# Contraction over pairs of time steps, and a scan's carry added by TensorE

## The chip, the cores and the metric

The kernel runs on one NeuronCore of a Trainium2 chip. The metric is the device time of one execution in microseconds (us). A core has five engines that run at the same time and wait for each other through semaphores: TensorE (PE, matmuls, with its weight loads shown as PEld), VectorE (DVE), ScalarE (ACT), GpSimd (POOL) and SyncE (SP), which here issues all DMAs. SBUF is the memory on the core with 128 partitions; PSUM is where PE writes, in 8 banks of 512 float32 per partition; PE adds there. GpSimd and DMA do not reach PSUM.

## The reference

Two layers with residuals over x of 4 x 1024 x 256 float32. The first is a selective scan:

```python
x = x + selective(layernorm(x))
# in selective, for batch b, channel d (256), state n (32), time t (1024):
dA    = exp(delta_t[:, :, None] * A[None])
dBu   = (delta_t * u_t)[:, :, None] * B_t[:, None, :]
h     = dA * h + dBu
y_t   = einsum('bdn,bn->bd', h, C_t)
...
y     = ys + u * D_param
```

delta, B and C come from projections of the normalised x. The second layer (`x + ffn(layernorm(x))`) has a two-tap convolution with SiLU, projections to queries, keys, values and gates, a routed attention whose length axis is the batch of four, a normalisation and an output projection.

## The kernel before

It has three stages. The first (P, to about 222 us) makes delta, delta times u, B and C, splits float32 numbers into bfloat16 terms and stores them in DRAM, with `base` = x + u D. The second (M, to about 850 us) is the scan. The third (F) is the second layer, over 8 tiles of 128 time steps.

In stage M the 128 partitions hold batch x state (4 x 32). Time goes in 32 chunks of 32 (`TC`); a chunk has two halves (`s`) of 16 time steps (`TS`), and a half has four groups `g` of 64 channels. One of these groups is called a step here: 8 a chunk, 256 in all, G being the step's number. Each step does this:

- PE, L1313: 8 bfloat16 matmuls write dBu for 64 channels x 16 time steps into one of two pairs of PSUM banks. They wait for the scan two steps back (L1308), which read that pair. `b_ready` counts them.
- PE, L1269 (`decay_args`): 8 bfloat16 matmuls write delta A for the next chunk. ACT takes the exponential (L1406) into `decay`.
- PE, L1282 (`contract`): y = C h for a half already scanned. The state is laid out channel by channel with the 16 time steps of a half adjacent, so that one time step of all 256 channels is a row of elements 16 apart. Each matmul takes one time step `t`: its stationary operand is 32 columns of `c_sta` (C of that time step, in 4 of the 32 columns, the rest zero), its output one of four 32-row blocks of PSUM, block `j` = t mod 4. Four of them run per step, side by side in the array. The columns of `c_sta` are placed so that row 4 q + b of block j gets time step 4 q + j of batch b; 8 rounds q accumulate over a chunk.
- POOL, L1163: `carry` = first decay of the step times the last state of the same channels in the half before. It waits for the scan four steps back. Then L1166 sets that first decay to 0, since one scan instruction runs over all 64 channels in a row.
- DVE, L1582: adds `carry` to the first time step of each channel in PSUM, and waits for itself. Then L1585: the scan over 64 x 16 elements.

Once a chunk POOL fills `c_sta` (L1140), ACT copies y from PSUM to `y_rows` (L1434), and SP stores it (`store_y`, L1032) with four DMAs, one for each block, as rows of 256 channels into `y_d`, which is laid out as batch, time, channel. SP also loads the inputs of the chunk after next (`load_md`, `load_mu`).

In stage F SP loads a tile of y and a tile of `base` with one DMA each (`f_load`, L295). POOL adds them (L368, `x1`), and later does gates (L380) and sums (L389) in the same queue. `phase_f_sync` gives the order on SP: the load of tile lt + 4, then the wait for tile lt's result and its store, then the load of tile lt + 5. The order within every engine is that of the code; nothing reorders it.

## Time and profile before

| | |
|---|---|
| device time, 3 runs | 1081.23, 1082.9, 1084.27 us (median 1082.9) |
| profiled execution, its own time | 1081.63 us |
| span of the profile | 1079.9 us |
| PE, DVE busy in the span | 85%, 81% |
| ACT, POOL busy in the span | 42%, 36% |
| mean granted clock of PE | 0.899 of full |

The span runs from the first to the last instruction of one profiled execution. A float32 matmul appears as two records (two passes), a bfloat16 one as one. In a view in order of time a row stands for several instructions of one line: its start, the time from the first start to the last end, and their count. Ends of matmuls overlap the next one, so the distance between two starts tells how long PE was taken. A granted clock of 1.00 is 2.4 GHz, 0.50 is 1.2 GHz.

### The profile page before, as it was taken

The page shows a single profiled execution, that of the slowest core. Times are in us where ns is not written, and L with a number is a line of the kernel's source. Part 1 is how long each engine was busy: PE and PEld are TensorE (multiplying, and loading weights), DVE is VectorE, ACT ScalarE, POOL GpSimd, SP SyncE. Part 2 cuts the span into 40 slices and gives each one's busy share as a digit, 9 for nine tenths or more (in the row PEclk, how much of TensorE's full clock was granted, in tenths as well). Part 3 has the DMA queues.
Part 4 walks back from the last instruction along what each step waited for, and adds up shares of the span by engine and source line. Part 5 has one row for each costly group of instructions (what it writes and reads, how often), then busy time and mean ns, then how long its engine had stood idle before and what let it go on. Part 6 is the DMA issues. An engine that isn't in the chain of part 4 may idle for free.

```text
span 1079.9 us, 22889 instructions
## 1 busy us (share of the span) xinstructions
PE 919.4 (85%) x7472; PEld 591.4 (55%) x7472; DVE 873.3 (81%) x1116; ACT 458.6 (42%) x807; POOL 384.4 (36%) x698
## 2 busy tenths in 40 slices
PE   5655462469999999999999999999999699777996
PEld 3433241346666666666666666666665377556774
DVE  6844575079999999999999999999999758455773
ACT  3444644424444444444444444444443244222531
POOL 6434643123333333333333333333335442333232
PEclk9655665579999999999999999999999999888997
DMA  9399998771121121111111211112114210111001
GB/s 327 59 152 175 209 130 138 125 125 59 53 63 53 52 65 53 60 58 51 63 54 50 65 53 60 56 53 63 53 51 143 70 58 1 59 59 59 21 20 59
DMA packets 206074, 85.76 MB, mean 79 GB/s; under 512 B 139221, under 2 KB 196053, under 8 KB 205269
## 3 DMA queue, kind: packets, MB, share of 16 engines
q1 hardware_dynamic: 206036, 85.30, 33.8%
q8 instruction: 19, 0.31, 0.1%
q14 instruction: 19, 0.15, 0.0%
HBM read 45.85 MB, written 39.42 MB: 79 GB/s over the span
## 4 chain that ended last, share of the span: by engine, by line
PE 63%; SPq 15%; issue 8%; DVE 7%; POOL 4%; ACT 2%; DMA 1%; ACTq 0%; POOLq 0%; DVEq 0%
PE psum L1282 23%; PE psum L1313 21%; PE psum L1269 10%; SPq L957 6%; SPq L1010 5%; PE psum L442 5%; DVE arena L1585 3%; POOL arena L389 2%; SPq L974 1%; PE psum L514 1%; SPq L951 1%; POOL arena L380 1%; PE psum L510 1%; POOL arena L368 1%; DMA delta_terms<-arena 0%
## 5 line engine op out<-in xcount | busy, mean ns | idle before, releaser
L1585 DVE TENSOR_TENSOR_SCAN arena<-arena,psum 128x1024 f32<-128x1024 f32 x256 | 585.4, 2287 | 8.8
L1406 ACT ACTIVATE arena<-psum 128x512 f32<-128x512 f32 x512 | 281.5, 604 | 349.6 <-PE psum L1269 308.0
L1313 PEld LDWEIGHTS psum<-du_mov,b_sta 96*128 96x128 bf16 x2048 | 200.3, 130 | 239.0 <-issue 214.1
L1313 PE MATMUL psum<-du_mov,b_sta 96*128 96x128 bf16 x2048 | 271.8, 313 | 20.2 <-DVE arena L1585 20.1
L1282 PE MATMUL psum<-arena,c_sta 128*32 128x256 f32 x2048 | 280.7, 629 | 2.3 <-DVE arena L1585 2.1
L1163 POOL TENSOR_TENSOR carry<-arena 128x64 f32<-128x64 f32 x252 | 119.0, 472 | 393.3 <-DVE arena L1585 384.6
L1269 PE MATMUL psum<-delta_mov,a_sta 96*128 96x128 bf16 x2048 | 171.7, 228 | 10.6 <-DMA delta_mov<-delta_terms 7.7
L1269 PEld LDWEIGHTS psum<-delta_mov,a_sta 96*128 96x128 bf16 x2048 | 151.9, 110 | 13.8 <-issue 8.1
L442 PE MATMUL psum<-delta_mov,arena 128*128 128x256 f32 (+6 forms) x544 | 119.9, 381 | 7.2 <-ACT arena L567 7.2
L442 PEld LDWEIGHTS psum<-delta_mov,arena 128*128 128x128 f32 x544 | 93.6, 205 | 28.4 <-ACT arena L567 8.2
L1582 DVE TENSOR_TENSOR psum<-psum,carry 128x64 f32<-128x64 f32 x256 | 55.1, 215 | 38.2 <-DMA delta_terms<-arena 38.2
L1166 POOL TENSOR_TENSOR arena<-zeros 128x64 f32<-128x64 f32 x256 | 78.1, 305 | 20.1
L1225 PE MATMUL psum<-arena 128*64 128x512 f32 x32 | 29.1, 1067 | 49.9 <-ACT arena L1354 49.9
L1282 PEld LDWEIGHTS psum<-arena,c_sta 128*32 128x32 f32 x2048 | 40.8, 108 | 31.5 <-issue 3.1
L811 DVE TENSOR_TENSOR arena<-arena 128x1024 f32<-128x1024 f32 x8 | 20.9, 2611 | 39.3 <-POOL arena L380 39.3
L1119 POOL TENSOR_TENSOR arena<-c_sta,arena 128x1024 f32<-128x1024 f32 x8 | 18.5, 2308 | 66.3 <-ACT arena L1393 66.3
L368 POOL TENSOR_TENSOR arena<-du_mov 128x1024 f32<-128x1024 f32 x8 | 18.8, 2356 | 64.5 <-DMA du_mov<-base 64.5
L1463 DVE BATCH_NORM_STATS2 arena<-arena 128x6 f32<-128x256 f32 x32 | 11.2, 410 | 37.6 <-DMA arena<-in_L_attn_x 37.6
L691 DVE TENSOR_TENSOR arena<-arena,psum 128x512 f32<-128x512 f32 (+3 forms) x32 | 14.5, 483 | 32.1 <-ACT delta_mov L583 19.1
L1225 PEld LDWEIGHTS psum<-arena 128*64 128x64 f32 x32 | 5.9, 213 | 62.7 <-ACT arena L1354 52.7
L389 POOL TENSOR_TENSOR arena<-arena 128x768 f32<-128x768 f32 (+2 forms) x24 | 36.0, 1500 | 8.9 <-DVE arena L745 6.6
L602 ACT ACTIVATE arena<-arena 128x1024 f32<-128x1024 f32 x8 | 8.5, 1057 | 63.9 <-POOL arena L389 63.9
(142 smaller groups left out, 777.1 us busy)
## 6 DMA issues: line engine op xcount, KB each, us to landing
du_terms<-arena SPq DMA_DIRECT2D x48, 256.0 KB, 3.9
du_mov<-du_terms SPq DMA_DIRECT2D x128, 96.0 KB
b_terms<-delta_mov SPq DMA_DIRECT2D x6, 1024.0 KB, 10.5
delta_terms<-arena SPq DMA_DIRECT2D x48, 128.0 KB, 5.2
delta_mov<-delta_terms SPq DMA_DIRECT2D x128, 48.0 KB
b_sta<-b_terms SPq DMA_DIRECT2D x64, 96.0 KB
arena<-in_L_attn_x SPq DMA_DIRECT2D x8, 512.0 KB, 5.6
base<-arena SPq DMA_DIRECT2D x8, 512.0 KB, 4.6
```

The source lines that it names most:

```text
L389: pool.tensor_tensor(o[:, 0:n], o[:, 0:n], arena[:, AV_TMP[m]:AV_TMP[m] + n], ALU.add)\
L442: mm = nc.tensor.matmul(psum[:, at:at + n], xc, w_all[:, h * WCOLS + col:h * WCOLS + col + n], start=(h == 0), stop=(h == 1))
L957: sp_.dma_start(dram(scratch_d, s * per_term + offset, *dims_), part(which)).then_inc(count, 16)
L1010: sp_.dma_start(dram(delta_terms_d, s * (B * L * D) + lt * (B * P * D) + h * (P * TC), (TC, P), (TC * D, B * P // TC), (1, TC)), dp_view(k ...
L1163: ins = pool.tensor_tensor(carry[:, g, :], seg[:, :, 0], before[:, :, TS - 1], ALU.mult)
L1166: pool.tensor_tensor(seg[:, :, 0], zeros[:, :], zeros[:, :], ALU.add)\
L1269: mm = nc.tensor.matmul(psum[:, (4 + u % 2) * BANK + i * P:(4 + u % 2) * BANK + (i + 1) * P], a_sta[0:ROWS, dg * P:(dg + 1) * P], sub(delt ...
L1282: mm = nc.tensor.matmul(psum[32 * j:32 * j + 32, (6 + k) * BANK:(6 + k) * BANK + D], c_sta[k][:, t * 32:(t + 1) * 32], sub(arena, 0, P, (2 ...
L1313: mm = nc.tensor.matmul(sub(psum, 0, P, o, (4, 4), (TS, GD // 2)), b_sta[k][0:ROWS, (s * 4 + tg) * P:(s * 4 + tg + 1) * P], sub(du_mov[k], ...
L1406: nc.scalar.activation(sub(arena, 0, P, k * CHUNK_ELEMS + u * 16 * TS, (TS, 16), (D * TS, SUBS), (1, TS)), sub(psum, 0, P, (4 + u % 2) * B ...
L1582: nc.vector.tensor_tensor(firsts, firsts, carry[:, g, :], ALU.add)\
L1585: nc.vector.tensor_tensor_scan(state[s][:, seg], decay[k][:, (s * D + g * GD) * TS:(s * D + (g + 1) * GD) * TS], psum[:, 2 * (step % 2) * ...
```

## The change

Three things are changed.

1. `contract` takes two adjacent time steps in one matmul (`TP` = 2): 512 columns, two adjacent elements out of every 16, with one stationary operand of 32 columns. Output block j of PSUM now holds two times 256 columns. A half has 2 rounds of 4 matmuls, where it had 4; they are placed in steps g = 1 and g = 3. A chunk has 4 rounds p. The matmul of round p and block j takes time steps 8 p + 2 j + u, u = 0 and 1. Its stationary operand holds C of both, in columns 8 p + 4 u + b for batch b, the rest zero; its output has two groups of 256 columns, one for each of the two states. So row 8 p + 4 u + b of block j holds y of its time step in column group u; what the other group holds there is not used. POOL fills `c_sta` with two operations (L1148 of the changed kernel), one for each u, with half the elements each.
2. y is copied whole (512 columns) and stored with one DMA a chunk, 128 rows of 2 KB, unused parts included. `f_load` picks the used parts with eight DMAs, each to 16 partitions 8 apart, and one for `base` (`YLOADS` = 9).
3. The carry is added by PE: after the 8 matmuls of L1313 (whose loops change places, halves outside) it waits for `carry_ready` and adds `carry` by two float32 matmuls with the identity as stationary operand, 32 columns each, in PSUM. DVE's addition and the semaphore `carried` go.

```diff
+TP = 2
+SETS = TS // (4 * TP)
+YROW = TP * D
+YLOADS = 4 * TP + 1
-        y_d = scratch("y", [B, L, D], F32)
+        y_d = scratch("y", [4, CHUNKS * 32, TP, D], F32)
-        y_rows = [sb(f"y_rows{k}", [P, D]) for k in range(2)]
+        y_rows = [sb(f"y_rows{k}", [P, 2 * D]) for k in range(2)]
...
         def f_load(eng, lt, k):
-            for tile, source in ((fraw[k], y_d), (fbase[k], base_d)):
-                eng.dma_start(tile.rearrange("p (b d) -> p b d", b=B),
-                              dram(source, lt * (P * D), (D, P), (L * D, B), (1, D))).then_inc(f_loaded[k], 16)
+            for j in range(4):
+                for u in range(TP):
+                    eng.dma_start(sub(fraw[k], TP * j + u, 16, 0, (D, B), (1, D), pstep=4 * TP),
+                                  dram(y_d, (j * CHUNKS * 32 + lt * P + u * B) * YROW + u * D,
+                                       (TP * B * YROW, 16), (YROW, B), (1, D))).then_inc(f_loaded[k], 16)
+            eng.dma_start(fbase[k].rearrange("p (b d) -> p b d", b=B),
+                          dram(base_d, lt * (P * D), (D, P), (L * D, B), (1, D))).then_inc(f_loaded[k], 16)
...
             def store_y(c, k):
-                for j in range(4):
-                    sp_.dma_start(dram(y_d, c * (TC * D) + j * D, (4 * D, TC // 4), (L * D, B), (1, D)),
-                                  y_rows[k][32 * j:32 * j + 32, :]).then_inc(y_stored[k], 16)
+                sp_.dma_start(dram(y_d, c * (32 * YROW), (CHUNKS * 32 * YROW, 4), (YROW, 32), (1, YROW)),
+                              y_rows[k][:, :]).then_inc(y_stored[k], 16)
...
-                    pool.tensor_tensor(
-                        sub(c_sta[k], 0, P, 0, (4 * 32 + 4, TC // 4), (32, 4), (1, B)),
+                    for u in range(TP):
+                        pool.tensor_tensor(
+                            sub(c_sta[k], 0, P, u * B, (4 * 32 + TP * B, 4), (32, 4), (1, B)),
...
                             if not early:
+                                pool.wait_ge(S["b_ready"], G - 3)
                                 pool.wait_ge(S["scan_done"], G - 3)
-                                pool.wait_ge(S["carried"], G - 3)
...
-            def contract(c, k, s, quads):
-                for qq in quads:
+            def contract(k, s, sets):
+                for r in sets:
                     for j in range(4):
+                        pi = SETS * s + r
                         mm = nc.tensor.matmul(
-                            psum[32 * j:32 * j + 32, (6 + k) * BANK:(6 + k) * BANK + D],
-                            c_sta[k][:, t * 32:(t + 1) * 32],
-                            sub(arena, 0, P, (2 * CHUNK_ELEMS + s * D * TS) + 4 * qq + j, (TS, D)),
+                            psum[32 * j:32 * j + 32, (6 + k) * BANK:(6 + k) * BANK + TP * D],
+                            c_sta[k][:, (pi * 4 + j) * 32:(pi * 4 + j + 1) * 32],
+                            sub(arena, 0, P, (2 * CHUNK_ELEMS + s * D * TS) + TP * (4 * r + j), (TS, D), (1, TP)),
...
-                            for tg in range(TS // 4):
-                                for half in range(2):
+                            for half in range(2):
+                                for tg in (1, 2, 3, 0):
...
+                            pe.wait_ge(S["carry_ready"], G + 1)
+                            for half in range(2):
+                                mm = nc.tensor.matmul(
+                                    sub(psum, 0, P, (pair_bank + half) * BANK, (TS, GD // 2)), ident[:, :],
+                                    carry[:, g, half * (GD // 2):(half + 1) * (GD // 2)],
+                                    start=False, stop=True, skip_group_check=True)
                             mm.then_inc(S["b_ready"], 1)
...
-                                if g == 0:
-                                    pe.wait_ge(S["scan_done"], G)
+                                if g == 1:
+                                    pe.wait_ge(S["scan_done"], G - 1)
...
-                                mm = contract(pc, pk, ps, [g])
+                                if g % 2 == 1:
+                                    mm = contract(pk, ps, [g // 2])
...
-                            firsts = sub(psum, 0, P, 2 * (step % 2) * BANK, (TS, GD))
-                            nc.vector.tensor_tensor(firsts, firsts, carry[:, g, :], ALU.add)\
-                                .then_inc(S["carried"], 1)
-                            dve.wait_ge(S["carried"], G + 1)
```

On PE, two steps of a chunk's inner loop, before (L1313 the inputs, L1269 the arguments, L1282 the contraction; REGISTER_ALU rows compute what a wait compares):

```order
L1313 MATMUL psum<-du_mov,b_sta 128x4x32 x8
L1266 REGISTER_ALU
L1269 MATMUL psum<-delta_mov,a_sta 128x128 x4
L1266 REGISTER_ALU
L1269 MATMUL psum<-delta_mov,a_sta 128x128 x4
L1282 MATMUL psum<-arena,c_sta 32x256 x4
L1308 REGISTER_ALU
L1313 MATMUL psum<-du_mov,b_sta 128x4x32 x8
L1266 REGISTER_ALU
L1269 MATMUL psum<-delta_mov,a_sta 128x128 x4
```

And in the changed kernel, where these are L1320, L1277 and L1289, and L1327 are the identity matmuls on `carry`:

```order
L1320 MATMUL psum<-du_mov,b_sta 128x4x32 x8
L1325 REGISTER_ALU
L1327 MATMUL psum<-carry,ident 128x32 x2
L1274 REGISTER_ALU
L1277 MATMUL psum<-delta_mov,a_sta 128x128 x4
L1274 REGISTER_ALU
L1277 MATMUL psum<-delta_mov,a_sta 128x128 x4
L1289 MATMUL psum<-arena,c_sta 32x512 x4
L1320 MATMUL psum<-du_mov,b_sta 128x4x32 x8
L1325 REGISTER_ALU
L1327 MATMUL psum<-carry,ident 128x32 x2
```

The contraction stands in every second step with twice the columns, and two identity matmuls stand behind the inputs in every step.

On SP, the end of stage M and the beginning of stage F, before (L1032 stores y, L295 loads y and base):

```order
L1032 DMA y<-y_rows 8x4x256 x4
L295 DMA du_mov<-y 128x4x256
L295 DMA du_mov<-base 128x4x256
L295 DMA du_mov<-y 128x4x256
L295 DMA du_mov<-base 128x4x256
L1032 DMA y<-y_rows 8x4x256 x8
```

And in the changed kernel (L1039 the store, L300 and L303 the loads):

```order
L1039 DMA y<-y_rows 4x32x512
L300 DMA du_mov<-y 16x4x256 x8
L303 DMA du_mov<-base 128x4x256
L300 DMA du_mov<-y 16x4x256 x8
L303 DMA du_mov<-base 128x4x256
L1039 DMA y<-y_rows 4x32x512 x2
```

A store has one DMA where it had four, a tile's load nine where it had two.

## Rows read from the trace of the kernel before

**Rows 1.** The page's first part: busy time, share of the span, instructions of each engine.

```profile
PE 919.4 (85%) x7472; PEld 591.4 (55%) x7472; DVE 873.3 (81%) x1116; ACT 458.6 (42%) x807; POOL 384.4 (36%) x698
```

**Rows 2.** Stages: us, then busy time (instructions) by engine, granted clock, DMA share, GB/s.

```profile
222.30:262.00 39.70, 37.19 (x341) 24.95 (x344) 39.11 (x34) 16.16 (x31) 12.69 (x33) 0.89 0.31 94
262.00:830.00 568.00, 568.00 (x5558) 342.46 (x5551) 560.03 (x463) 262.22 (x493) 191.57 (x529) 1.00 0.18 58
830.00:850.40 20.40, 17.48 (x137) 8.27 (x135) 20.12 (x18) 1.15 (x3) 15.45 (x28) 1.00 0.31 103
```

**Rows 3.** Lines, 300 to 800 us: form, count, busy us, mean ns, idle before.

```profile
L1585 DVE TENSOR_TENSOR_SCAN arena<-arena,psum 128x1024 f32<-128x1024 f32 x205 | 468.8, 2287 | 7.1
...
L1282 PE MATMUL psum<-arena,c_sta 128*32 128x256 f32 x1632 | 224.1, 629 | 0.0
...
L1269 PE MATMUL psum<-delta_mov,a_sta 96*128 96x128 bf16 x1632 | 132.9, 224 | 0.0
```

**Rows 4.** Order of time, 502 to 505 us: start, us, what, count, idle before.

```profile
502.03 0.43 POOL L1163 TENSOR_TENSOR carry<-arena 128x64 f32<-128x64 f32 x1 [1.63 <-DVE arena L1585]
...
502.11 2.29 DVE L1585 TENSOR_TENSOR_SCAN arena<-arena,psum 128x1024 f32<-128x1024 f32 x1
502.11 1.08 PE L1282 MATMUL psum<-arena,c_sta 128*32 128x256 f32 x8
...
503.13 1.05 PE L1313 MATMUL psum<-du_mov,b_sta 96*128 96x128 bf16 x8
...
503.97 0.65 PE L1269 MATMUL psum<-delta_mov,a_sta 96*128 96x128 bf16 x8
504.31 0.21 DVE L1582 TENSOR_TENSOR psum<-psum,carry 128x64 f32<-128x64 f32 x1
...
504.55 1.12 PE L1282 MATMUL psum<-arena,c_sta 128*32 128x256 f32 x8
504.56 2.29 DVE L1585 TENSOR_TENSOR_SCAN arena<-arena,psum 128x1024 f32<-128x1024 f32 x1
```

**Rows 5.** Other float32 matmuls on PE in order of time, then the clock there.

```profile
66.05 3.67 PE L1225 MATMUL psum<-arena 128*64 128x512 f32 x4 [7.64 <-ACT arena L1354]
69.65 1.10 PE L1234 MATMUL psum<-arena 128*32 128x128 f32 x16
70.69 1.97 PE L1240 MATMUL psum<-arena 128*128 128x32 f32 x16
...
945.38 1.88 PE L510 MATMUL psum<-arena,ident 128*128 128x512 f32 x4
947.10 3.62 PE L514 MATMUL psum<-delta_mov,arena 128*128 128x256 f32 x16
...
69.60:70.60 1.00, 1.00 (x17) 0.65 (x16) 0.00 (x0) 0.58 (x1) 0.00 (x0) 0.50 0.98 320
70.68:72.70 2.02, 1.98 (x20) 1.86 (x16) 0.93 (x3) 0.00 (x0) 0.00 (x0) 1.00 1.14 164
```

**Rows 6.** PE in order of time, two groups of the first steps.

```profile
226.28 1.14 PE L1269 MATMUL psum<-delta_mov,a_sta 96*128 96x128 bf16 x8
227.22 1.91 PE L1313 MATMUL psum<-du_mov,b_sta 96*128 96x128 bf16 x8
```

**Rows 7.** PE in order of time, the contraction behind the last scan.

```profile
850.43 3.90 PE L1282 MATMUL psum<-arena,c_sta 128*32 128x256 f32 x32 [0.41 <-DVE arena L1585]
```

**Rows 8.** A load of the last stage; then SP's issues, ns min/median/max.

```profile
952.27 0.51 SPq L295 DMA_DIRECT2D du_mov<-y  x1
...
958.69 2.34 POOL L368 TENSOR_TENSOR arena<-du_mov 128x1024 f32<-128x1024 f32 x1 [18.97 <-DMA du_mov<-base]
...
L295 SPq DMA_DIRECT2D du_mov<-y x8: 367/474/507, 828.1 to 982.5; - x8
...
DMA to landing us min/median/max: 3.5/5.8/7.3
...
L1032 SPq DMA_DIRECT2D y<-y_rows x128: 656/677/790, 253.1 to 856.9; - x128
```

More of the change, by code:

```diff
@@ L122, in bank @@
             return psum[:, i * BANK:(i + n) * BANK]
[L125 removed]
+        names = """own_made b_filled a_sta_zeroed c_sta_zeroed wv_sum wv_mean
             wv_centred weights_loaded ident_zeroed ident_ready zeros_ready wT_psum wT_ready a_exp a_neg a_hi
@@ L277, in m_done @@
             for k in range(2):
-                eng.wait_ge(y_stored[k], 16 * 4 * (CHUNKS // 2))
+                eng.wait_ge(y_stored[k], 16 * (CHUNKS // 2))
         def dims(t, off, *d):
@@ L364, in x1 @@
             def x1(lt):
-                pool.wait_ge(f_loaded[lt % 2], 32 * (lt // 2 + 1))
+                pool.wait_ge(f_loaded[lt % 2], 16 * YLOADS * (lt // 2 + 1))
                 if lt >= FY:
@@ L1139, in m_pair @@
                         pool.wait_ge(S["contract_done"], 2 * c - 2)
-                    pool.tensor_tensor(
-                        sub(c_sta[k], 0, P, 0, (4 * 32 + 4, TC // 4), (32, 4), (1, B)),
-                        c_all[:, bass.ds(c * TC, TC)].rearrange("p (q j) -> p q j", j=4)
-                        .unsqueeze(3).to_broadcast([P, TC // 4, 4, B]),
-                        sub(own_batch, 0, P, 0, (0, TC // 4), (0, 4), (1, B)), ALU.mult)\
-                        .then_inc(S["cpad_ready"], 1)
+                    for u in range(TP):
+                        pool.tensor_tensor(
+                            sub(c_sta[k], 0, P, u * B, (4 * 32 + TP * B, 4), (32, 4), (1, B)),
+                            c_all[:, bass.ds(c * TC, TC)].rearrange("p (q j u) -> p q j u", j=4, u=TP)[:, :, :, u]
+                            .unsqueeze(3).to_broadcast([P, 4, 4, B]),
+                            sub(own_batch, 0, P, 0, (0, 4), (0, 4), (1, B)), ALU.mult)\
+                            .then_inc(S["cpad_ready"], 1)
                     for s in range(SUBS):
@@ L1274, in decay_args @@
                 return mm
-            def contract(c, k, s, quads):
-                for qq in quads:
+            def contract(k, s, sets):
+                for r in sets:
                     for j in range(4):
-                        t = s * TS + 4 * qq + j
-                        q = t // 4
+                        pi = SETS * s + r
                         mm = nc.tensor.matmul(
-                            psum[32 * j:32 * j + 32, (6 + k) * BANK:(6 + k) * BANK + D],
-                            c_sta[k][:, t * 32:(t + 1) * 32],
-                            sub(arena, 0, P, (2 * CHUNK_ELEMS + s * D * TS) + 4 * qq + j, (TS, D)),
-                            start=(q == 0), stop=(q == TC // 4 - 1), skip_group_check=True)
+                            psum[32 * j:32 * j + 32, (6 + k) * BANK:(6 + k) * BANK + TP * D],
+                            c_sta[k][:, (pi * 4 + j) * 32:(pi * 4 + j + 1) * 32],
+                            sub(arena, 0, P, (2 * CHUNK_ELEMS + s * D * TS) + TP * (4 * r + j), (TS, D), (1, TP)),
+                            start=(pi == 0), stop=(pi == SETS * SUBS - 1), skip_group_check=True)
                 return mm
@@ L1337, in _ @@
             pe.wait_ge(S["scan_done"], CHUNKS * STEPS)
-            contract(CHUNKS - 1, 1, 1, range(4)).then_inc(S["contract_done"], 1)
+            contract(1, 1, range(SETS)).then_inc(S["contract_done"], 1)
             phase_f_pe(pe)
@@ L1409, in exps, with y_copy @@
                     .then_inc(S["exp_done"], 1)
+            def y_copy(k):
+                nc.scalar.copy(y_rows[k].rearrange("p (u d) -> p u d", u=TP),
+                               sub(psum, 0, P, (6 + k) * BANK, (1, TP), (TP, D))).then_inc(S["y_evac"], 1)
             for u in range(UNITS):
@@ L1432, in m_pair @@
                             if not (isinstance(n, int) and n <= 0):
-                                act.wait_ge(y_stored[1 - k], 64 * n)
-                            nc.scalar.copy(y_rows[1 - k][:, :],
-                                           bank(7 - k)[:, 0:D])\
-                                .then_inc(S["y_evac"], 1)
+                                act.wait_ge(y_stored[1 - k], 16 * n)
+                            y_copy(1 - k)
             m_pair(0, True, False)
@@ L1445, in _ @@
             act.wait_ge(S["contract_done"], 2 * CHUNKS)
-            act.wait_ge(y_stored[1], 64 * (CHUNKS // 2 - 1))
-            nc.scalar.copy(y_rows[1][:, :], bank(7)[:, 0:D]).then_inc(S["y_evac"], 1)
+            act.wait_ge(y_stored[1], 16 * (CHUNKS // 2 - 1))
+            y_copy(1)
             phase_f_act(act)
```

5 lines of the change are left out of this document (2 added, 3 removed).

## The prediction, made before the changed kernel was run

> **What bounds the kernel now.** I read the page's first part, then the stages, the costliest lines, and the order of time inside one step. The page gives PE 85% and DVE 81% of a 1079.9 us span [rows 1]. The stages show where: from 262 to 830 us PE is busy 568.00 of 568 and DVE 560.03, at the full clock (2.4 GHz), while ACT and POOL are under half and DMA takes 0.18 [rows 2]. So this is a loop with two nearly full engines, and 85% against 81% does not say which of them sets the pace. The lines from 300 to 800 us hold 204 steps, 2.451 us each (500/204), each with one scan of 2287 ns [rows 3].
>
> Inside a step [rows 4]: scan starts 502.11, next L1582 starts 504.31, next scan 504.56. A scan therefore holds DVE for 2.20 us, and the addition with its wait for itself costs 0.25. DVE shows no idle time. PE starts the contraction at 502.11, the state inputs (L1313) at 503.13, the exponents' arguments (L1269) at 503.97 and the next contraction at 504.55: 1.02, 0.84 and 0.58, no gap between them. Over many steps the contraction averages 2.451 − 0.84 − 0.58 = 1.03. Both engines sum to 2.45: taking work from DVE alone would gain nothing, PE's new sum decides. ACT is under half full; POOL computes a carry right after a scan (502.03), for a scan four steps later.
>
> **DVE.** 256 additions leave. DVE's floor becomes 2.20 a step.
>
> **PE, what goes.** Half a chunk (four steps) had four groups of four contractions over 256 columns, each a matmul in two passes; now two groups over 512, in every second step. What a 512-column pass takes is the disputed number. In one group (32 matmul records, four groups, eight passes in 3.90 us) a 256-column pass takes (3.90 − 0.63)/7 = 0.47 [rows 7, 3]; in the loop, from the x8 row, (1.08 − 0.63) = 0.45 [rows 4]. Other float32 matmuls at full clock: L514, 256 adjacent columns, 3.62/16 = 0.23, a little less without the last record's overhang; L510, 512 columns, (947.10 − 945.38)/4 = 0.43 [rows 5]. The contraction's columns thus cost double. It differs in two ways: four 32-column tiles run side by side, and it picks one element out of every 16 (64 bytes). The tiles are not the cause as far as a row shows: L1234 runs four tiles of 128 adjacent columns in (70.69 − 69.65)/4 = 0.26, and L1225 at the same half clock (granted 0.50) needs (69.65 − 66.05)/4 = 0.90 for 512 columns in one stream, 0.23 for 128 [rows 5]. So the stride is what is left. The change reads two adjacent elements per 64 bytes. No row shows that form: a 512-column pass lies between 0.43 (adjacent) and 0.90 (as now). I take 0.43 plus the 0.03 that a pass carries now (0.46), because the doubling looks like one extra access time per separate piece, and there are half as many pieces. A group then costs what it costs today, 1.03, and there are half as many. At the upper end it costs 1.03 + 2 × 0.43 = 1.89.
> The Trainium skill, "SBUF — State Buffer", section "Door 1: The DMA port swizzle", says that SBUF lines are 16 bytes long and that at least two accesses to a line are needed for full bandwidth. By that rule one element per 64 bytes is slow and two adjacent ones are at full speed (a group of 1.03); without it, nothing but my reading of the stride supports the halving (1.89 remains possible). Its penalty for single elements agrees with 0.45 against 0.23.
>
> **PE, what comes.** Two identity matmuls of 32 columns per step, two passes each, so four weight loads of 128 × 128 float32. L1240 has this very form at the full clock: 16 records in 1.97, the last about 0.28 long, so 1.69/15 = 0.113 [rows 5]. Four are 0.45. I take 0.43, since the last of the L1313 matmuls already holds PE for 0.11 while the first identity is loaded. Bounds: 0.11, if loads were hidden and only the columns counted (4 × 32 columns at 0.23/256); 0.86, if each pass took what a 256-column one takes. The writes go to PSUM 64 bytes apart, as those of L1313, which cost 0.84/8 = 0.11 per 128 against 0.06 for L1269; for 32 columns that stays below the load. The order of L1313 (halves outside) moves nothing: the same eight loads and writes; between 0 and a doubled 0.11 each I take 0. The new wait, for the carry, sits ahead of the identity matmuls, and behind it are the arguments and the contraction, for which ACT and DVE wait. POOL has the carry ready about 0.5 after the scan four steps back, and the inputs wait for a scan two steps back, so it costs nothing. In the last chunk POOL also turns keys between carries, which eats into a lead of two steps but not all of it; a loss there would be a step or so, and I take 0.
>
> **The step.** Arguments before a contraction cost 0.58; without one behind them 8 × 0.061 = 0.49 (0.65 less the last record's 0.22 [rows 3, 4], over 7). Two steps: 0.84 + 0.43 + 0.49 + 0.84 + 0.43 + 0.58 + 1.03 = 4.64, so 2.32 per step against DVE's 2.20. PE is then the bound. The contraction in one lump does not stall it: the input for a step may start when the scan two back is over. Count from the start of an even step's input: its scan starts at 0.84 + 0.43 + 0.28 = 1.55, the odd one's 2.20 later at 3.75, so the odd scan before that started at −0.89 and ended at 1.40, and PE comes to the odd input only at 1.76. All 256 steps but the first four and the last eight run in this form: 244 × (2.451 − 2.323) = −31.2.
>
> **The ends.** (1) The first four steps run at half clock: an input group takes about 1.6 and arguments 227.22 − 226.28 = 0.94 [rows 6]; with about 0.5 more PE is behind DVE, +0.4. (2) The last seven intervals have no arguments, PE needs 2.32 less about 0.5 and DVE sets them: 7 × 0.25 = −1.7. (3) The last contraction, on the chain, took 3.90 for four groups [rows 7]; two remain, −1.9, and its copy to `y_rows` is twice as wide, +0.2. (4) In the last stage SP loads y and base for tile lt + 4 only behind the output of tile lt. POOL sits idle for 18.97 us until base lands, and the gates and sums behind it go through POOL [rows 8]; tiles 5, 6 and 7 all wait like this, so three loads are on the path. From y's issue to x1 is 6.4 (952.27 to 958.69). Now there are eight y issues ahead of base's. One issue lies between 0.37 and 0.68 in the rows [rows 8]; I take 0.45 and 0.04 between, so base starts 3.9 after instead of 0.55. It no longer shares the engines with a whole y: a load alone landed in as little as 3.5 [rows 8], so 3.9 + 3.6 = 7.5 and a loss of 1.1, at worst (0.68 each) 2.9, at best 0. With what the issue of base itself may add I take 1.5, three times, and 0.5 for tile 2: +5.0. SP's y stores fall from four to one a chunk; it was not the bound. ACT's wider copy (0.2 more) and POOL's second c_sta operation fit in their idle time.
>
> Sum: 1081.6 (the profiled execution, 1.7 over its span, 1.3 under the median of 1082.9, inside their range) − 31.2 + 0.4 − 1.7 − 1.7 + 5.0 = 1052.4, say **1052**.
>
> **Rivals.** *Pairs read no faster.* A group costs 1.89 and two steps 5.50, 2.75 each: 244 × 0.30 = +73; the last intervals −1.2, the tail +0.1, first steps and loads as above: **1159**, slower. For it: every strided read of state here has the same stride, so nothing separates piece from element. Against: adjacent columns run at twice the rate. It decides from a group of 1.27 (passes of 0.58), where the whole comes out even. *Identity matmuls dearer*, 0.86 instead of 0.43: 2.75 per step, about **1157**; half of that is 1105. For it: float32 weights between bfloat16 ones occur nowhere in the loop. Against: L1240 is the same form. *They are hidden*: with 0.19 or less a step PE sums under 2.20 and DVE sets it: −61, **1023**. For it: L1313 is slow for another reason than weights, so loads might slip beneath. Against: L1240 shows loads as the rate at 32 columns.
>
> **Numbers.** Forecast 62% (its own range 1035 to 1073, from 0.36 to 0.52 for the identity passes), hidden 13%, pairs no faster 14%, dearer identities 11%. The range 1018 to 1095 holds the forecast, the hidden case and the mild part of dearer identities; pairs without gain are left out. About 3 us either way, 0.3%, cannot be told from no change here. Faster: 62 + 12; same: 4, from the mild dear case; slower: 22.
>
> **What would show it.** After the change: steps of 4.6 in pairs; 512-column passes of 0.46 (right) or 0.9 (wrong); the input start to the arguments start 1.27 instead of 0.84; DVE idle about 0.1 a step waiting for PE, where before it had none; DVE without idle time means the hidden case. In the last stage POOL's waits for base grow by 1 to 2 us each. A granted clock below full in the loop would make the prediction wrong, as would PE waiting on POOL's carry.

## The result, and the profile after

| | before | after |
|---|---|---|
| device time, median (lowest to highest) | 1083.59 us (1081.23 to 1086.44), 4 runs | 1052.51 us (1050.63 to 1056.41), 4 runs |
| ratio of after to before, 95% interval | | 0.9717 [0.9678, 0.9756] |
| the profiled execution | 1081.63 us, span 1079.9 | 1050.63 us, span 1048.9 |

Executions over 1.5% above the fastest of the same kernel are left out of the ratios, here and in the experiments. 31.0 us left the profiled execution. The page's first part for the kernel after, with each engine's busy time and its share of the span (before: [rows 1]):

```profile
PE 883.2 (84%) x7472; PEld 672.1 (64%) x7472; DVE 824.1 (79%) x860; ACT 462.5 (44%) x807; POOL 379.6 (36%) x730
```

PE lost 36 us of work and DVE 49, and both shares look as before; where the time went is to be read from the stages. Loop and first steps of the kernel after; the columns are those of [rows 2] (duration, busy time of PE, PEld, DVE, ACT and POOL, granted clock, DMA share, GB/s):

```profile
222.30:262.00 39.70, 38.82 (x338) 31.90 (x338) 34.04 (x16) 15.68 (x29) 12.15 (x34) 0.80 0.28 84
262.00:800.00 538.00, 537.21 (x5632) 415.64 (x5632) 525.33 (x237) 266.49 (x494) 195.73 (x576) 1.00 0.24 71
```

In the loop PE is full, as before, and DVE now has 12.7 us of idle time in 538. PE is the bound. The costliest lines from 300 to 780 us (before: [rows 3]), with count, busy time, mean ns of one, idle time ahead and who ended it:

```profile
L1597 DVE TENSOR_TENSOR_SCAN arena<-arena,psum 128x1024 f32<-128x1024 f32 x211 | 470.4, 2273 | 11.5 <-PE psum L1327 5.9
...
L1289 PE MATMUL psum<-arena,c_sta 128*32 128x512 f32 x840 | 121.0, 640 | 0.0
L1327 PE MATMUL psum<-carry,ident 128*128 128x32 f32 x844 | 120.7, 266 | 0.0
```

The scan is what it was. The identity matmuls have as much busy time as the whole contraction, which has 105 groups of 8 passes. Two steps in order of time (before: [rows 4]):

```profile
500.13 6.73 DVE L1597 TENSOR_TENSOR_SCAN arena<-arena,psum 128x1024 f32<-128x1024 f32 x3 [0.23 <-PE psum L1327]
...
500.21 1.04 PE L1320 MATMUL psum<-du_mov,b_sta 96*128 96x128 bf16 x8
...
501.05 0.57 PE L1327 MATMUL psum<-carry,ident 128*128 128x32 f32 x4
...
501.45 0.61 PE L1277 MATMUL psum<-delta_mov,a_sta 96*128 96x128 bf16 x8
...
502.00 1.12 PE L1289 MATMUL psum<-arena,c_sta 128*32 128x512 f32 x8
...
503.05 1.05 PE L1320 MATMUL psum<-du_mov,b_sta 96*128 96x128 bf16 x8
...
503.89 0.57 PE L1327 MATMUL psum<-carry,ident 128*128 128x32 f32 x4
...
504.30 0.61 PE L1277 MATMUL psum<-delta_mov,a_sta 96*128 96x128 bf16 x8
...
504.75 0.71 PE L1320 MATMUL psum<-du_mov,b_sta 96*128 96x128 bf16 x5
```

From start to start on PE: inputs 0.84, identities 0.40, arguments 0.55, contraction 1.05 over 512 columns, then inputs 0.84, identities 0.41 and arguments 0.45. DVE runs three scans without a gap and waited 0.23 for the identity matmuls ahead of them. Over many steps a group takes 1.055 or 1.116, 1.085 in the mean, and two steps are 4.57.

Marked by the starts of the scans, the profiled executions differ as follows. An interval is the time from one scan's start to the next one's; the forecast of a row is the prediction's terms laid on the same marks (0.128 gained in each of 244 intervals, 8 of them in the second row and 8 in the fourth).

| | before | after | difference | forecast |
|---|---|---|---|---|
| to the first scan | 222.34 | 220.84 | −1.5 | 0 |
| first 12 intervals | 29.44 | 32.58 | +3.1 | −0.6 |
| next 228 intervals | 2.454 each | 2.283 each | −39.0 | −29.2 |
| last 15 intervals | 36.75 | 33.54 | −3.2 | −2.7 |
| last scan to the end | 231.83 | 241.35 | +9.5 | +3.3 |
| sum | | | −31.0 | −29.2 |

The first row lies ahead of the loop that the change touches; over all the profiles here it varies from 217.8 to 225.0 with no order by kernel, so it is the spread of single executions. Of the others the loop gave 10 us more than forecast, and the two ends took 10 back.

**First steps.** In the kernel after, in order of time:

```profile
226.41 1.92 PE L1320 MATMUL psum<-du_mov,b_sta 96*128 96x128 bf16 x8
...
228.04 0.98 PE L1327 MATMUL psum<-carry,ident 128*128 128x32 f32 x4
...
228.83 1.04 PE L1277 MATMUL psum<-delta_mov,a_sta 96*128 96x128 bf16 x8
...
229.66 1.92 PE L1320 MATMUL psum<-du_mov,b_sta 96*128 96x128 bf16 x8
...
235.63 2.29 DVE L1597 TENSOR_TENSOR_SCAN arena<-arena,psum 128x1024 f32<-128x1024 f32 x1 [0.94 <-PE psum L1327]
...
236.31 1.94 PE L1289 MATMUL psum<-arena,c_sta 128*32 128x512 f32 x8
```

And the clock there (columns as above):

```profile
230.00:236.00 6.00, 6.00 (x39) 6.00 (x38) 4.07 (x3) 1.66 (x5) 1.96 (x6) 0.50 0.17 53
236.00:238.00 2.00, 2.00 (x12) 0.31 (x10) 1.92 (x1) 1.07 (x2) 0.00 (x0) 0.50 0.00 0
238.00:262.00 24.00, 24.00 (x254) 18.77 (x250) 21.89 (x10) 11.34 (x21) 7.99 (x22) 0.99 0.22 65
```

A step takes 3.25 (226.41 to 229.66): 1.63 for the inputs, 0.79 for the identities, 0.83 for the arguments, with no gap on PE, and the scan waits 0.94 for it. The granted clock is 0.50 (1.2 GHz) until 238 us, although PE is busy without a break from 223.2 on. In the kernel before PE was busy from 224.7 on, with no gap over 0.15, and the clock rose at 231.1 (0.74 in the mean of 230 to 232).

**Last stage.** SP and POOL after the output of tile 1, in order of time (before: [rows 8]):

```profile
913.98 0.38 SPq L318 DMA_DIRECT2D out<-arena  x1
914.41 5.33 SPq L300 DMA_DIRECT2D du_mov<-y  x8
...
919.78 0.59 SPq L303 DMA_DIRECT2D du_mov<-base  x1
924.14 2.34 POOL L376 TENSOR_TENSOR arena<-du_mov 128x1024 f32<-128x1024 f32 x1 [22.30 <-DMA du_mov<-base]
```

From the store of a tile to the `x1` that waits for the load behind it (the load of tile 5 stands behind the store of tile 0, and so on) are 10.9, 10.2 and 10.0 us for tiles 5, 6 and 7, and were 8.3, 6.8 and 7.0.

### The profile page after: what moved, and what is told of

It reads as the page before. It is cut to its first block, busy times and chain, and to the rows that moved or that the text cites. A ratio compares the mean times of both kernels' runs of the same rounds, so it can differ in the third digit from the quotient of the medians.

```text
span 1048.9 us, 22555 instructions
## 1 busy us (share of the span) xinstructions
PE 883.2 (84%) x7472; PEld 672.1 (64%) x7472; DVE 824.1 (79%) x860; ACT 462.5 (44%) x807; POOL 379.6 (36%) x730
## 4 chain that ended last, share of the span: by engine, by line
PE 65%; SPq 15%; issue 9%; DVE 4%; POOL 4%; ACT 2%; DMA 1%; ACTq 0%; POOLq 0%; DVEq 0%
PE psum L1320 22%; PE psum L1289 13%; PE psum L1277 11%; PE psum L1327 9%; SPq L965 6%; PE psum L450 6%; SPq L1018 5%; POOL arena L397 2%; DVE arena L1597 2%; SPq L982 1%; PE psum L522 1%; SPq L959 1%; PE psum L518 1%; POOL arena L388 1%; POOL arena L376 1%
## 5 line engine op out<-in xcount | busy, mean ns | idle before, releaser
L1597 DVE TENSOR_TENSOR_SCAN arena<-arena,psum 128x1024 f32<-128x1024 f32 x256 | 570.6, 2273 | 58.0 <-DMA delta_terms<-arena 39.6
L1420 ACT ACTIVATE arena<-psum 128x512 f32<-128x512 f32 x512 | 278.1, 595 | 308.3 <-PE psum L1277 304.5
L1320 PEld LDWEIGHTS psum<-du_mov,b_sta 96*128 96x128 bf16 x2048 | 206.2, 131 | 136.1 <-DVE arena L1597 133.2
L1320 PE MATMUL psum<-du_mov,b_sta 96*128 96x128 bf16 x2048 | 272.1, 314 | 19.0 <-DVE arena L1597 19.0
L1171 POOL TENSOR_TENSOR carry<-arena 128x64 f32<-128x64 f32 x252 | 110.8, 440 | 361.5 <-DVE arena L1597 270.8
L1277 PE MATMUL psum<-delta_mov,a_sta 96*128 96x128 bf16 x2048 | 163.2, 224 | 12.5 <-DMA delta_mov<-delta_terms 9.7
L1277 PEld LDWEIGHTS psum<-delta_mov,a_sta 96*128 96x128 bf16 x2048 | 143.9, 110 | 15.7 <-issue 10.0
L1327 PE MATMUL psum<-carry,ident 128*128 128x32 f32 x1024 | 148.8, 269 | 0.0
L1327 PEld LDWEIGHTS psum<-carry,ident 128*128 128x128 f32 x1024 | 148.1, 206 | 0.0
L1289 PE MATMUL psum<-arena,c_sta 128*32 128x512 f32 x1024 | 148.0, 643 | 0.0
L450 PE MATMUL psum<-delta_mov,arena 128*128 128x256 f32 (+6 forms) x544 | 119.7, 380 | 7.1 <-ACT arena L575 7.1
L450 PEld LDWEIGHTS psum<-delta_mov,arena 128*128 128x128 f32 x544 | 93.6, 205 | 28.9 <-issue 8.9
L376 POOL TENSOR_TENSOR arena<-du_mov 128x1024 f32<-128x1024 f32 x8 | 18.8, 2351 | 74.9 <-DMA du_mov<-base 74.8
L511 PE MATMUL psum<-ident,arena 128*128 128x128 f32 x64 | 11.9, 349 | 34.5 <-DVE arena L819 33.2
```

The source lines that it names most:

```text
L450: mm = nc.tensor.matmul(psum[:, at:at + n], xc, w_all[:, h * WCOLS + col:h * WCOLS + col + n], start=(h == 0), stop=(h == 1))
L1171: ins = pool.tensor_tensor(carry[:, g, :], seg[:, :, 0], before[:, :, TS - 1], ALU.mult)
L1277: mm = nc.tensor.matmul(psum[:, (4 + u % 2) * BANK + i * P:(4 + u % 2) * BANK + (i + 1) * P], a_sta[0:ROWS, dg * P:(dg + 1) * P], sub(delt ...
L1289: mm = nc.tensor.matmul(psum[32 * j:32 * j + 32, (6 + k) * BANK:(6 + k) * BANK + TP * D], c_sta[k][:, (pi * 4 + j) * 32:(pi * 4 + j + 1) * ...
L1320: mm = nc.tensor.matmul(sub(psum, 0, P, o, (4, 4), (TS, GD // 2)), b_sta[k][0:ROWS, (s * 4 + tg) * P:(s * 4 + tg + 1) * P], sub(du_mov[k], ...
L1327: mm = nc.tensor.matmul(sub(psum, 0, P, (pair_bank + half) * BANK, (TS, GD // 2)), ident[:, :], carry[:, g, half * (GD // 2):(half + 1) * ...
```

## Experiments

Each line number in an edit is that of the kernel after or before that it starts from; a run with one time is a single execution, and the kernel before took 1084.8 us in a single execution beside the first four.

**1. What makes the contraction cheap: adjacent elements, one 16-byte piece, or neither?** `arena` holds 4 bytes an element, so the two elements of a pair lie in one aligned 16-byte piece. Three kernels change only which two elements a matmul reads, so their y is not the reference's. In e3_across_line blocks 2 and 3 read the same elements, and both rounds of a half read the same.

```diff
-  sub(arena, ..., TP * (4 * r + j), (TS, D), (1, TP)),
+  sub(arena, ..., 4 * r + j, (TS, D), (8, TP)),              # e1_apart: 32 bytes apart
+  sub(arena, ..., 4 * j + r, (TS, D), (2, TP)),              # e2_same_line: 8 apart, one piece
+  sub(arena, ..., 4 * min(j, 2) + 3, (TS, D), (1, TP)),      # e3_across_line: adjacent, two pieces
```

> The changed kernel, but the two time steps of a contraction lie 8 elements (32 bytes) apart instead of side by side; 512 columns as before. y comes from other time steps than it should. Theory A (a column costs double when it stands alone in its 16 bytes): a 512-column pass takes 0.9 us instead of the 0.46 of the changed kernel, a group 1.9 to 2.0, two steps 4.57 + 0.86 = 5.43, and the time rises by 122 x 0.86 = 105 us to about 1157 us. Theory B (the old contraction was slow because of its many small groups and tiles side by side, not because of its stride): the pass stays at 0.46 and the time at 1052 us.

> The changed kernel, but the two time steps of a contraction are elements 0 and 2, or 1 and 3, of an aligned group of four (same 16 bytes, not adjacent). y comes from other time steps than it should. Theory A (16 bytes count): as fast as adjacent ones, a pass 0.46 us, the time 1052 us. Theory C (adjacency counts, a separate piece costs double): a pass 0.9 us, the time about 1157 us.

> The changed kernel, but the two time steps of a contraction are adjacent elements on either side of a 16-byte border (3 and 4, 7 and 8, 11 and 12). y comes from other time steps than it should. Theory A (16 bytes count): a pass 0.9 us, the time about 1157 us. Theory C (adjacency counts): a pass 0.46 us, the time 1052 us.

Measured: 1159.48, 1041.24 and 1157.92 us. The contraction and the group behind it on PE, e1_apart first:

```profile
499.84 2.02 PE L1289 MATMUL psum<-arena,c_sta 128*32 128x512 f32 x8
501.79 1.05 PE L1320 MATMUL psum<-du_mov,b_sta 96*128 96x128 bf16 x8
```

Then e2_same_line:

```profile
502.84 1.07 PE L1289 MATMUL psum<-arena,c_sta 128*32 128x512 f32 x8
503.84 1.05 PE L1320 MATMUL psum<-du_mov,b_sta 96*128 96x128 bf16 x8
```

And e3_across_line:

```profile
501.37 2.04 PE L1289 MATMUL psum<-arena,c_sta 128*32 128x512 f32 x8
503.34 1.05 PE L1320 MATMUL psum<-du_mov,b_sta 96*128 96x128 bf16 x8
```

A group takes 1.95, 1.00 and 1.97; from the start of its first matmul record to that of its fifth, which is one pass, are 0.906, 0.457 and 0.867. Adjacency doesn't matter: two elements with a gap between them are fast in one 16-byte piece, and two neighbours across its border are as slow as two that lie apart. So the halving came from the piece, and the first rival ("pairs read no faster") describes just what these two slow kernels do: they sit at its 1159. The rule of the Trainium skill, "SBUF — State Buffer", section "Door 1: The DMA port swizzle", that lines are 16 bytes and want two accesses each, is borne out here for TensorE's moving operand (0.457 against 0.906 and 0.867).

e2_same_line was also 11 us faster than the kernel after. Its pass is a constant 0.457, while that of the kernel after is 0.459 in one group and 0.510 in the next. The difference between the two: in the kernel after, the matmuls of blocks 0 and 1, and those of blocks 2 and 3, read two halves of the same 16 bytes from two tiles of the array, with starts 0.007 apart; in e2_same_line each tile has pieces of its own. Experiment 7 uses that. In the two slow kernels tiles share pieces too; no run here separates that from their pairs being split, but in the kernel after sharing by two tiles costs at most 0.05 a pass, against the 0.41 to 0.45 in question.

**2. What the carry costs on PE, and where DVE's floor is.** The identity matmuls and their wait are left out, and with them the carry from half to half.

```diff
-  pe.wait_ge(S["carry_ready"], G + 1)
-  for half in range(2):
-      mm = nc.tensor.matmul(sub(psum, ...), ident[:, :], carry[:, g, ...], ...)
```

> The changed kernel without the two identity matmuls and their wait: the carry is left out of the scan. PE then needs (4.57 - 2 x 0.41)/2 = 1.88 us a step. Theory A (PE's sum sets the changed kernel's pace of 2.283): DVE takes over at 2.20, the loop gains 244 x 0.08 = 20 us and the slow first steps 3 us more, about 1030 us, with no DVE idle time in the loop. Rival (DVE or POOL already sets the pace): no change, 1050 us.

Measured: 1021.48 us, 2.178 a step, below both the 2.20 and the 1030 us that were expected. DVE and PE in order of time:

```profile
498.44 8.79 DVE L1591 TENSOR_TENSOR_SCAN arena<-arena,psum 128x1024 f32<-128x1024 f32 x4
...
502.94 1.05 PE L1320 MATMUL psum<-du_mov,b_sta 96*128 96x128 bf16 x8 [0.44 <-DVE arena L1591]
```

Now DVE runs without a gap and PE waits for it. This is the forecast's "hidden" case, made real: 1023 was its time. The first 12 intervals take 26.53 instead of 32.58, 6.0 less, of which the loop's gain (12 × 0.105) explains 1.3; the other 4.8 are what the identities cost there, with their own time at the half clock and with a half clock that lasts longer (see the end of the section on the prediction).

**3. Each half of the change alone.** e5_pairs_only is the kernel after with the carry added by DVE as before. e6_carry_only is the kernel before with the carry on PE. The semaphore that POOL's carry waits for changes with them.

```diff
 # e5_pairs_only, from the kernel after
-  (the wait for carry_ready and the two identity matmuls)
+  nc.vector.tensor_tensor(firsts, firsts, carry[:, g, :], ALU.add).then_inc(S["carried"], 1)
+  dve.wait_ge(S["carried"], G + 1)
 # e6_carry_only, from the kernel before: the same lines the other way round
```

> The contraction in pairs and y stored whole, but the carry added by DVE as before. Theory A (before, both engines were full; PE relieved alone gains nothing): DVE stays at 2.20 + 0.24 a step, so 2.44 to 2.45, the last contraction saves 2 us and the y loads of the last stage cost 9: 1083.6 + 5 = 1088 us, 0.4% slower than before. Rival (before, PE set the pace and DVE's additions were slowed by it): the step falls to 2.3 or less and the time to 1055 us.

> The kernel before, with the carry added by PE and the contraction in single time steps, y stored as before. Theory A: PE needs 0.83 + 0.41 + 0.54 + 1.05 = 2.83 us a step, 244 x 0.38 = +93 us and some 4 us in the first steps: about 1178 us. Rival (DVE set the pace before, PE had room that its records hide): not over 1100 us.

Measured: 1087.67 us (1082.68 to 1090.21, 10 runs), ratio 1.0023 [1.0004, 1.0042], for the pairs; 1176.85, ratio 1.0845 [1.0817, 1.0873], for the carry. In e5_pairs_only:

```profile
500.38 0.21 DVE L1592 TENSOR_TENSOR psum<-psum,carry 128x64 f32<-128x64 f32 x1
500.52 1.05 PE L1320 MATMUL psum<-du_mov,b_sta 96*128 96x128 bf16 x8 [0.76 <-DVE arena L1595]
500.62 2.29 DVE L1595 TENSOR_TENSOR_SCAN arena<-arena,psum 128x1024 f32<-128x1024 f32 x1
```

And in e6_carry_only, where L1320 are the identity matmuls:

```profile
501.19 2.29 DVE L1587 TENSOR_TENSOR_SCAN arena<-arena,psum 128x1024 f32<-128x1024 f32 x1 [0.43 <-PE psum L1320]
501.46 1.12 PE L1282 MATMUL psum<-arena,c_sta 128*32 128x256 f32 x8
```

With the pairs alone PE idles (0.76 before the inputs) behind a DVE that still needs 2.45 a step, and the slower last stage (240.97 from the last scan to the end, against 231.83) is what is left. With the carry alone DVE idles behind a PE that needs 2.84. PE's relief is worth nothing without DVE's, and DVE's, bought with work on PE, costs 8% without PE's: the gain is a property of both together. That is what [rows 2] said with two full engines.

**4. The last stage.** e7_one_y_load fetches y with one DMA, as before, of rows that are not the tile's y; everything else is the kernel after.

```diff
-  for j in range(4):
-      for u in range(TP):
-          eng.dma_start(sub(fraw[k], TP * j + u, 16, ...), dram(y_d, ...))
+  eng.dma_start(fraw[k].rearrange("p (b d) -> p b d", b=B), dram(y_d, lt * (P * D), (D, P), ...))
```

> The changed kernel, but in the last stage a tile of y is loaded by one DMA of the same bytes with base's pattern, so it holds the wrong rows. Theory A (the eight small loads cost the three waits of POOL 3 us each): 9 to 10 us less, about 1043 us. Rival (the last stage is longer for another reason, such as the lower clock of its first transposes): 1052 us.

Measured: 1044.52 us, ratio 0.9641 [0.9602, 0.968]. From the last scan to the end it takes 231.99, against 241.35 after and 231.83 before. SP and POOL after the output of tile 1:

```profile
911.54 0.38 SPq L315 DMA_DIRECT2D out<-arena  x1
...
912.51 1.05 SPq L300 DMA_DIRECT2D du_mov<-base  x1
918.34 2.35 POOL L373 TENSOR_TENSOR arena<-du_mov 128x1024 f32<-128x1024 f32 x1 [19.09 <-DMA du_mov<-base]
```

6.8 from the store to `x1`, where it was 10.2. So the eight loads are the whole loss of the last stage, 9.4 us, and the shorter last contraction gave nothing that can be seen there: the result of tile 0 is stored 72.2 us after the start of the last scan in the kernel before (920.31) and after (879.77) alike.

**5. The wait for the load itself.** Both kernels issue the load of tile lt + 5 only behind the output of tile lt. Here every load from tile 4 on is issued two tiles earlier, so those of tiles 4, 5 and 6 stand ahead of the first output.

```diff
   load(3)
+  load(4)
+  load(5)
   for lt in range(LT):
-      if lt + 4 < LT: load(lt + 4)
+      if lt + 6 < LT: load(lt + 6)
```

> The kernel before, with SP issuing the loads of tiles 5, 6 and 7 of the last stage two tiles earlier, ahead of the stores of results 0 and 1. Theory A (POOL's waits of 19 to 21 us for them are on the path, three times): at least the way from the store to the addition goes, 8.3 + 6.8 + 7.0 = 22 us, about 1061 us or less. Rival (POOL's idle time is cover for PE, and only its end counts): less than 3 us, 1081 us or more.

> The changed kernel with the loads of tiles 5, 6 and 7 issued two tiles earlier. Theory A (they are on the path with 10.9 + 10.2 + 10.0 us): about 1052.5 - 31 = 1021 us or less, and the 9 us that the eight small loads cost are gone with it. Rival (only what the small loads added is on the path): 1043 us.

Measured: from the kernel before 1055.29 us, ratio 0.9711 [0.9674, 0.9748]; from the kernel after 1012.81 (1005.78 to 1022.37), ratio 0.9291 [0.9235, 0.9347]. From the last scan to the end: 201.68 and 199.18. POOL's `x1` in the first of them, by line, from 850 us on:

```profile
L370 POOL TENSOR_TENSOR arena<-du_mov 128x1024 f32<-128x1024 f32 x7 | 16.5, 2358 | 5.0 <-DMA du_mov<-base 5.0
```

And in the kernel before, without that edit, over the whole span:

```profile
L368 POOL TENSOR_TENSOR arena<-du_mov 128x1024 f32<-128x1024 f32 x8 | 18.8, 2356 | 64.5 <-DMA du_mov<-base 64.5
```

POOL's wait for `base` falls from 64.5 us to 5.0, and in e9_early from 74.8 to 7.0. The first results now lie 20.5 us apart, where they lay 30.3 to 31.5 apart before and 33.3 to 34.2 after, and the nine DMAs of a tile cost nothing that can be seen. Two lines moved in the order of SP are worth as much to the kernel before as the whole change under study.

**6. The clock of the first steps.** Sixteen float32 matmuls of 512 columns, whose results nobody uses, are put on PE ahead of the third step, into a bank that is free there: in the kernel after (e10_fill) and with experiment 5's edit (e11_early_fill).

```diff
+  if first and k == 0 and step == 2:
+      for _ in range(16):
+          nc.tensor.matmul(bank(6), ident[:, :], c_all[:, 0:BANK], start=True, stop=True)
```

> The changed kernel with 16 float32 matmuls of 512 columns, whose result nobody reads, on PE ahead of the third step of the scan stage, where PE sits idle for 19 us. Theory A (the first steps of the scan are slow because PE runs at half clock until 238 us and its sum with the identity matmuls is over DVE's): steps 1 to 6 fall from 2.8 to 4.2 us to 2.3, about 6 us less, 1046 us. Rival (the steps wait for DMA or for ACT): no change. If the matmuls last longer than the idle time they cost up to 5 us instead.

> Both: the loads of tiles 5 to 7 earlier and the 16 filling matmuls, on the changed kernel. The two act in different stages, so their gains should add: about 1015 us if both theories hold.

Measured: 1048.7 us, ratio 0.9661 [0.9613, 0.971], and 1007.43 (1003.94 to 1012.0), ratio 0.9282 [0.9244, 0.932]. The first can't be told from the kernel after (0.9717 [0.9678, 0.9756]), nor the second from e9_early (0.9291). Both are inconclusive as times. The clock row of e10_fill:

```profile
230.00:238.00 8.00, 8.00 (x49) 6.14 (x47) 5.48 (x3) 2.23 (x5) 2.37 (x7) 0.50 0.15 51
```

and of e11_early_fill:

```profile
222.00:230.00 8.00, 8.00 (x20) 3.61 (x19) 4.46 (x2) 0.00 (x0) 1.46 (x4) 1.00 0.82 239
230.00:238.00 8.00, 7.37 (x76) 6.50 (x75) 5.87 (x3) 3.25 (x6) 1.91 (x6) 1.00 0.18 65
```

In e10_fill the added matmuls were over at 220.4, before the first scan at 221.4; PE then idled for 3.3 us, and the clock fell back to 0.50 at 225.1. In e11_early_fill they reached into the loop: the clock stayed at 1.00, but they held the third step up once by 4.7 us, and the first 12 intervals took 31.49 against 36.83 in e9_early.

**7. The version that the runs point to.** The kernel after with: pairs whose four tiles read pieces of their own (experiment 1), `c_sta`, `y_d` and its stores laid out to match, so that a tile's y comes with two DMAs instead of eight, and a chunk is again stored with four; the early loads (5); the added matmuls (6).

```diff
-  sub(arena, ..., TP * (4 * r + j), (TS, D), (1, TP)),
+  sub(arena, ..., 4 * j + TP * r, (TS, D), (1, TP)),
-  y_d = scratch("y", [4, CHUNKS * 32, TP, D], F32)
+  y_d = scratch("y", [CHUNKS * P, TP, D], F32)
...
+  for u in range(TP):
+      eng.dma_start(sub(fraw[k], u, 64, 0, (D, B), (1, D), pstep=TP),
+                    dram(y_d, (lt * 4 * P + u * B) * YROW + u * D, (TP * B * YROW, 64), (YROW, B), (1, D)))
```

> A correct version of all findings: pairs are given to the four tiles so that they read in four different 16-byte pieces (block j takes elements 4 j + 2 r + u of a half), y is stored in an order in which a tile is loaded by two DMAs and one for base, loads of tiles 5 to 7 early, 16 filling matmuls. Theory D (two tiles that read in the same 16 bytes slow each other: pass 0.485 us in the changed kernel, 0.458 in e2 with a piece for each tile): the pass is 0.458, the step 2.24 instead of 2.283, 244 x 0.043 = 10 us less than e11's 1007.4: about 997 us. Rival (e2 was fast because its two elements are not adjacent): the pass stays at 0.485 and the time at 1007 us.

Measured: 995.87 us (987.9 to 1008.8, 6 runs), ratio 0.9177 [0.914, 0.9214]. In order of time:

```profile
499.77 6.86 DVE L1603 TENSOR_TENSOR_SCAN arena<-arena,psum 128x1024 f32<-128x1024 f32 x3
...
501.73 1.07 PE L1292 MATMUL psum<-arena,c_sta 128*32 128x512 f32 x8
502.73 1.05 PE L1326 MATMUL psum<-du_mov,b_sta 96*128 96x128 bf16 x8
```

The group is 1.00 and a step 2.240, as in e2_same_line, now with the reference's y. The first 12 intervals take 26.61 at a clock of 1.00, and it is 200.42 from the last scan to the end. Against e11_early_fill the 228 middle intervals give 9.9 us and the first twelve 4.9. The 4.9 are partly luck: the added matmuls ended at 217.9, just as the first scan began, PE idled for 2.2 us behind them, and the clock did not fall, as it had in e10_fill. This is the fastest kernel here, ahead of both.

## Why the prediction came out right

The total, 1052 against 1052.5, is better than its terms. Step by step:

- **The bound.** PE was to become the bound with DVE idle about 0.1 a step. PE is full, DVE idles 12.7 us over 237 scans, 0.05 each; in stretches it waits 0.23 and then not for three scans. Against DVE's own pace of 2.178 (e4_no_carry) a step of 2.283 leaves 0.105. Right. That relieving PE alone gives nothing is shown by e5_pairs_only. e6_carry_only (+8%) shows what the carry costs PE without the pairs; that a relief of DVE which costs PE nothing would give nothing either follows from PE being full, and no run tests it.
- **The 512-column pass.** 0.46 was taken between bounds of 0.43 and 0.90; it is 0.485 in the mean, the group 1.085 for 1.03. The sharing of pieces between tiles, of which the prediction had no term, fits the difference (e12_own_lines: 0.457 and 1.00). The reason given, one access time for each separate piece, was right only with "piece" read as an aligned 16 bytes (e3_across_line). Adjacent columns, on which the prose leaned, aren't the cause.
- **Identity matmuls.** 0.407 for 0.43. The row with the same form was a good measure, and neither "hidden" nor "dearer" happened.
- **Arguments.** 0.45 and 0.54 for 0.49 and 0.58: sized too high.
- **The step.** These make 4.57 for 4.64 in two steps. The term of −31.2 for 244 intervals was thus too small: 0.171 instead of 0.128 in each, −41.7. It started from a mean of 2.451 that PE and DVE both filled, and a small error in the new sum (0.04 in 2.32) is a third of a gain of 0.13. That is the term's weakness: a difference of two nearly equal numbers.
- **First steps.** +0.4 was mis-sized; on the table's marks the error is 3.7 us. Its own figures give more: 1.6 + 0.94 and 0.5 for the identities are 3.04 a step, 0.6 over 2.45, which is some 2.4 in four steps. And 0.5 was too little, since the identities take 0.79 at half clock, so that a step took 3.25. Besides, the half clock lasted to 238.5 us instead of 231.1, over five intervals of 2.83 to 4.19; that it would last as long as before was assumed without being said. e4_no_carry shows that the identities make the loss; e12_own_lines that at full clock it isn't there.
- **The last contraction.** −1.7 was nearly lost. The rows, of the kernel after:

```profile
807.56 2.26 DVE L1597 TENSOR_TENSOR_SCAN arena<-arena,psum 128x1024 f32<-128x1024 f32 x1
...
809.31 1.06 PE L426 MATMUL psum<-delta_mov 128*128 128x16 f32 x8 [0.68 <-ACT delta_mov L549]
...
810.31 1.97 PE L1289 MATMUL psum<-arena,c_sta 128*32 128x512 f32 x16
...
813.07 2.07 ACT L560 ACTIVATE arena<-arena,delta_mov 128x256 f32<-128x256 f32 x4 [0.15 <-DVE delta_mov L681]
...
815.20 1.89 PE L443 MATMUL psum<-ident,arena 128*128 128x128 f32 x8 [2.92 <-ACT arena L560]
820.24 10.06 PE L450 MATMUL psum<-delta_mov,arena 128*128 128x128 f32 x37 [3.15 <-ACT arena L575]
```

  and of the kernel before, behind [rows 7]:

```profile
856.79 1.09 PE L435 MATMUL psum<-ident,arena 128*128 128x128 f32 x8 [2.47 <-ACT arena L552]
861.17 9.13 PE L442 MATMUL psum<-delta_mov,arena 128*128 128x128 f32 x34 [3.29 <-ACT arena L567]
```

  The contraction shrank from 3.90 to 1.97 as said, but it starts 2.75 after the start of the last scan, where it was 2.34 (the scan began at 848.09): PE is still with L426. And it no longer ends the wait of ACT's L560 (L552 in the kernel before), which feeds the transposes: DVE's L681, the end of the statistics of that layer, is what L560 waits for now. So the transposes (L443) start 7.64 after the last scan where it was 8.70, 1.06 earlier. They then take 1.89 instead of 1.09, at a granted clock of 0.53 from 815 to 820 us, against 0.76 from 856 to 862 before, and L450 starts only 0.4 earlier. The prediction had the contraction alone on this path, and the clock at no price.
- **The loads.** The mechanism was right and the size off: 2.7, 3.3 and 3.0 for three tiles where 1.5 was taken each, 9.4 in all (e7_one_y_load) for 5.0. For tile 6 `base` is issued 5.37 behind the first issue of y (914.41 to 919.78), eight issues of 0.67 in the mean, where 0.45 + 0.04 each, 3.9 in all, was expected; that alone is 1.45. And from the issue of `base` to `x1` are 4.36 (919.78 to 924.14), where 3.6 was expected: 0.76. With the 1.1 of the prediction these are the 3.3. "At worst 2.9" was the better number. The prediction has a slip in its words here: it is the load of tile lt + 5, not lt + 4, that stands behind the output of tile lt; its three waits are the right ones.

So the loop's surplus of 10 and the ends' shortfall of 10 cancelled. The forecast's place (PE the bound, faster by 3%) was earned by the sum of the step; its last digits were luck.

**The longer half clock.** It comes with the identities in every profile. From the start of the first scan to the rise of the clock are 8.8 us in the kernel before, and 6.7, 6.8 and 9.1 in the other kernels without them (e4_no_carry, e5_pairs_only, e8_before_early). In the kernel after they are 17.7, and in the other kernels with them, but for the three with added matmuls, 14.3 to 26.6 (14.3 in e6_carry_only, 17.2 to 19.0 in e1_apart, e2_same_line, e3_across_line and e7_one_y_load, 26.6 in e9_early). In each, PE is busy from 2.3 us behind that start until the clock rises, with no gap over 0.15.

What stays open: why the clock stays down longer with the identity matmuls on PE; why it lasted 9 us longer in e9_early, whose first steps have the same code as the kernel after (36.83 for the first 12 intervals against 32.58); and the cause of the pass being 0.459 or 0.510. That the shared 16 bytes make it is argued from two kernels that share nothing (e2_same_line, e12_own_lines) and have it constant, not seen directly.

## What to carry to other kernels

When two engines are equally full, an edit that relieves one is worth nothing by itself (e5_pairs_only), and one that relieves it by loading the other costs in full (e6_carry_only): price both sums per step, as a pair. When a matmul reads with a stride, count the aligned 16-byte pieces it touches and not the elements. Ahead of any change to a transfer at a queue's end, look for whether it could be issued earlier: here that was worth as much as the change. And a sum made at full clock doesn't hold for steps that run at half clock; price those with rows of their own.

## What the runs showed of the hardware

- At full clock a float32 pass over 512 strided columns takes 0.457 us with two elements of each aligned 16-byte piece, adjacent or not, and 0.87 to 0.91 with one.
- In the kernel whose column tiles read halves of the same pieces at the same time a pass takes 0.459 or 0.510; in the two whose tiles have pieces of their own it takes 0.457 every time.
- The granted clock stayed at 0.50 for 15 us (223.2 to 238.5) in which PE was busy throughout with small matmuls, the identities among them; without the identities it rose after 6.4 us of such work in the kernel before.
- Scans over 1024 elements that DVE runs back to back start 2.178 apart, though a single one is recorded with 2.29.
- SP needs 0.67 in the mean from one issue of a load to 16 partitions to the next; the issue of a load of a whole tile (0.51 to its end, 0.55 to the next) is hardly cheaper, so eight small ones take SP almost ten times as long as one large one (5.37 against 0.55).
